# A bidirectional selective scan with a routed FFN gate: the projection kept in float32, one more state scaled on ScalarE, five scan buffers, another prologue

## What is computed

```python
xn = _layernorm(x, axis=-1)

def _selective_scan(x, x_proj_w, dt_proj_w, dt_proj_b, A_log, Dp):
    A = -jnp.exp(A_log)
    dbc = jnp.einsum('bld,nd->bln', x, x_proj_w)
    delta, Bm, Cm = jnp.split(dbc, [DT_RANK, DT_RANK + D_STATE], axis=-1)   # 32, 16, 16
    delta = jax.nn.softplus(jnp.einsum('blr,dr->bld', delta, dt_proj_w) + dt_proj_b)
    deltaA = jnp.exp(delta[..., None] * A)
    BX = delta[..., None] * Bm[:, :, None, :] * x[..., None]
    ...   # h[t] = deltaA[t] * h[t-1] + BX[t] along the tokens
    y = jnp.einsum('blds,bls->bld', hs, Cm)
    return y + Dp * x

s = scan_forward(xn) + scan_backward(xn)
# the FFN, with the expert sel of the row (8 experts, 256 -> 512 -> 256):
h = gelu(einsum('bsh,bhf->bsf', xn, W1[sel]) + b1[sel])
out = (einsum('bsf,bfh->bsh', h, W2[sel]) + b2[sel]) @ Wo + bo
x = x + s * silu(xn + 0.3 * out)
```

## Time and profile before

| | |
|---|---|
| median of 3 runs | 3154.97 us (3154.29 to 3155.58) |
| the profiled execution's own time | 3155.45 us |
| its span | 3153.7 us |
| VectorE busy | 3030.7 us (96%) |
| GpSimd busy | 3013.3 us (96%) |
| ScalarE busy | 2942.1 us (93%) |
| TensorE busy (matmul / weight load) | 2540.5 (81%) / 2013.5 us (64%) |
| mean granted TensorE clock | 0.943 |

### The profile page before, as it was taken

The page is one execution under the profiler, slowest core; times in us unless marked ns, Lnnn a source line. Parts: engine busy times, 40 slices in busy tenths (PEclk is TensorE's granted clock), DMA queues, the critical chain, the costliest instruction groups (busy, mean ns, idle before and its releaser), DMA issues. The chain is left out here.

```text
span 3153.7 us, 49209 instructions
## 1 busy us (share of the span) xinstructions
PE 2540.5 (81%) x15990; PEld 2013.5 (64%) x15990; DVE 3030.7 (96%) x1995; ACT 2942.1 (93%) x5242; POOL 3013.3 (96%) x1486
## 2 busy tenths in 40 slices
PE   7788778888788788788888788887888887887886
PEld 5666666666666666666666666666666665666665
DVE  2899999999999999999999999999999999999998
ACT  4899999999999999999999999999999999999995
POOL 2799999999999999999999999999999999999997
PEclk9999999999999999999999999999999999999998
DMA  5543344443344443444443444443444433444331
GB/s 158 151 123 124 104 130 140 132 126 120 110 129 139 131 118 119 122 131 138 125 122 111 126 139 135 124 121 109 128 142 131 120 121 117 129 139 130 109 121 54
DMA packets 273364, 394.17 MB, mean 125 GB/s; under 512 B 45003, under 2 KB 119508, under 8 KB 273108
## 3 DMA queue, kind: packets, MB, share of 16 engines
q1 hardware_dynamic: 273108, 391.03, 41.4%
HBM read 348.98 MB, written 25.18 MB: 119 GB/s over the span
## 5 line engine op out<-in xcount | busy, mean ns | idle before, releaser
L480 POOL TENSOR_TENSOR bx<-dx,b_sb 128x1024 f32<-128x1024 f32 x576 | 1362.4, 2386 | 22.0 <-DVE hs L861 21.8
L861 DVE TENSOR_TENSOR_SCAN hs<-decay,bx 128x1024 f32<-128x1024 f32 x576 | 1311.7, 2282 | 29.1 <-POOL hc L468 20.8
L468 POOL TENSOR_TENSOR hc<-hs,c_sb 128x1024 f32<-128x1024 f32 x480 | 1133.2, 2371 | 13.5 <-DVE hs L861 12.9
L1093 PE MATMUL y<-ident,hc 128*128 128x128 f32 x8192 | 1112.3, 285 | 36.9 <-DVE hc L840 36.9
L1093 PEld LDWEIGHTS y<-ident,hc 128*128 128x128 f32 x8192 | 977.2, 146 | 151.8 <-DVE hc L840 107.3
L861 DVE TENSOR_TENSOR_SCAN hs<-decay_sb,decay 128x1024 f32<-128x1024 f32 x448 | 1007.3, 2273 | 18.3 <-issue 13.8
L736 ACT ACTIVATE decay<-delta,rate 128x512 f32<-128x512 f32 x1152 | 748.1, 687 | 71.7 <-DVE hs L861 71.3
L594 ACT ACTIVATE dxb<-dxT,btok 128x256 f32<-128x256 f32 x1792 | 763.5, 508 | 0.1
L1068 PE MATMUL decay<-ident,dxb 128*128 128x128 f32 x3584 | 476.5, 276 | 238.3 <-DVE hs L861 219.1
L840 DVE TENSOR_TENSOR hc<-hs,c 128x1024 f32<-128x1024 f32 x544 | 652.0, 1199 | 0.6 <-issue 0.6
L1068 PEld LDWEIGHTS decay<-ident,dxb 128*128 128x128 f32 x3584 | 396.0, 141 | 395.3 <-issue 252.2
(11 more groups left out here) (125 smaller groups left out, 2066.0 us busy)
## 6 DMA issues: line engine op xcount, KB each, us to landing
b_sb<-b_scratch SPq DMA_DIRECT2D x576, 256.0 KB, 3.3
c_sb<-b_scratch SPq DMA_DIRECT2D x480, 256.0 KB, 3.6
xin<-in_L_attn_x_dram SPq DMA_DIRECT2D x32, 512.0 KB, 6.2
w_sb<-in_L_ffn_W_dram SPq DMA_DIRECT2D x32, 512.0 KB, 3.4
w2o_sb<-w2o_scratch SPq DMA_DIRECT2D x32, 512.0 KB
xres<-in_L_attn_x_dram SPq DMA_DIRECT2D x32, 512.0 KB, 5.4
out_dram<-og SPq DMA_DIRECT2D x32, 512.0 KB, 4.3
dbc<-high SPq DMA_DIRECT2D x64, 128.0 KB, 2.3
```

The lines of the kernel that those rows point to most:

```text
L468: nc.gpsimd.tensor_tensor(hc[:, s % RING, :, :], hs[:, s % HSLOTS, :, :], c_sb[:, i % CRING, :].unsqueeze(1).broadcast_to([P, DT, T]), ALU ...
L480: nc.gpsimd.tensor_tensor(bx[:, i % RING, :, :], dx[:, g, :, :], b_sb[:, i % BRING, :].unsqueeze(1).broadcast_to([P, DT, T]), ALU.mult).th ...
L861: V.tensor_tensor_scan(hs[:, s % HSLOTS, :, :].rearrange("p k t -> p (k t)")[:, u], factor.rearrange("p k t -> p (k t)")[:, u], data.rearr ...
L1093: ins = M(yps[:, c, k * P:(k + 1) * P], hc[:, s % RING, k, c * P:(c + 1) * P], ident[:, :], start=False, stop=(s == ADDED[-1]), is_transpo ...
```

## The change

- `high`, `low`, `dbc` and the selector are gone, with the activation, the VectorE subtraction and the four DMAs per row that made them. `projected` gets two buffers, by the row's parity. ScalarE's one copy waits that the stores and the C broadcasts of two rows before are done with it. Expands are one float32 matmul each and the C broadcasts take a column of the identity; both read `projected`.
- State 12 joins `TURNED`, with its scaling at step 8 by the new `SCALED_AT` entries (7 for state 12 and 8 for 13); GpSimd does 17 states of bx in place of 18. dxb has four slots in place of three. The decay of state 8 is made at step 5. The scaling of state 15 moves from step 10 to 11. GpSimd's first log1p of the next row moves from step 25 to 26.
- hs has five slots in place of four, taken in turn across rows.
- In the prologue W2^T has two buffers in hc; the last tokens' load has a semaphore of its own, and ScalarE's work on the row and its first transposed copy stand before that on the last tokens. SyncE reads the router's index after the store of expert 2, not of expert 3. On TensorE the four expands come before expert 4, the bias too, and the hidden parts lie among experts 6 and 7, where they stood before expert 5. Gelu stands before the copies of expert 7 and the second decay, and the dx turns and their copies come behind.

```diff
-    HSLOTS = 4
+    HSLOTS = 5
-    TSLOTS, XSLOTS = 3, 3
+    TSLOTS, XSLOTS = 3, 4
-    LOG1P, STEPSIZE, DX, CUT = (25, 36), (27, 39), (28, 43), (29, 44)
+    LOG1P, STEPSIZE, DX, CUT = (26, 36), (27, 39), (28, 43), (29, 44)
-    TURNED, SCALED_AT, TURN_LEAD = (5, 6, 8, 9, 11, 13, 14, 15, 22, 24, 26, 28, 29, 30), (1, 2, 3, 4, 5, 7, 9, 10, 17, 19, 21, 23, 24, 25), 3
+    TURNED, SCALED_AT, TURN_LEAD = (5, 6, 8, 9, 11, 12, 13, 14, 15, 22, 24, 26, 28, 29, 30), (1, 2, 3, 4, 5, 7, 8, 9, 11, 17, 19, 21, 23, 24, 25), 3
-    AHEAD, AHEAD_NEXT = {14: 22, 15: 24, 16: 26, 23: 28, 26: 29, 27: 30}, {29: 5}
+    AHEAD, AHEAD_NEXT = {5: 8, 14: 22, 15: 24, 16: 26, 23: 28, 26: 29, 27: 30}, {29: 5}
...
-            def high_part(row):
+            def copy_projected(row, par):
                 act.wait_ge(s_pf, row * UNITS + 3)
 
-                wait(act, s_dbc, row * 64)
-                A(high[:, :], fps[:, :], ACT.Copy).then_inc(s_hi, 1)
-
-                wait(act, s_bstored, row * 32)
-                A(projected[:, :], fps[:, :], ACT.Copy).then_inc(s_proj, 1)
+                wait(act, s_bstored, (row - 1) * 32)
+                wait(act, s_cps, (row - 1) * ND)
+                A(projected[:, par, :], fps[:, :], ACT.Copy).then_inc(s_proj, 1)
...
-            def turn_b(row):
-
-                pe.wait_ge(s_lo, row + 1)
+            def turn_b(row, par):
+
                 pe.wait_ge(s_proj, row + 1)
...
-                if q == 0:
-                    pe.wait_ge(s_dbc, row * 64 + 64)
-                M(fps[:, :], dtw_high[:, g, k, :], dbc[:, par, g, :], start=True, stop=False)
-                M(fps[:, :], dtw_low[:, g, k, :], dbc[:, par, g, :], start=False, stop=True).then_inc(s_pf, 1)
+                M(fps[:, :], dtw[:, g, k, :], projected[:, par, :], start=True, stop=True).then_inc(s_pf, 1)
...
-                g, n = s // N, s % N
-                M(cps[:, :], selector[:, N + n:N + n + 1].broadcast_to([P, P]), dbc[:, par, g, :], start=True, stop=True).then_inc(s_cps, 1)
+                at = s // N * 64 + R + N + s % N
+                M(cps[:, :], ident[:, at:at + 1].broadcast_to([P, P]), projected[:, par, :], start=True, stop=True).then_inc(s_cps, 1)
...
             def turn_w2(e):
 
                 pe.wait_ge(s_w2[e % 2], e // 2 * 16 + 16)
+                wait(pe, s_w2Tc, 2 * e)
```

More of the change, by code:

```diff
@@ L167, in mamba_moe_block @@
         w2_in = (w2o_sb, xres)
-        w2T_sb = hc[:, 0, :, :]
-        w2T = w2T_sb.rearrange("p a (j k f) -> p (a j) k f", k=DT, f=P)
+        w2T_sb = [hc[:, a, :, :] for a in range(2)]
+        w2T = [w2T_sb[a].rearrange("p a (j k f) -> p (a j) k f", k=DT, f=P) for a in range(2)]
         w2o_st = (og, zz)
@@ L332, in load_residual, with store_bc @@
                 sp.dma_start(xres[:, :, :], one(x_rows, row)).then_inc(s_xr, 16)
[L334 to L341, removed]
+            def store_bc(row, par):
                 wait_alone(sp, s_proj, row + 1)
                 for g in range(2):
-                    sp.dma_start(b_dram[par, g], projected[64 * g + R:64 * g + 64, :]).then_inc(s_bstored, 16)
+                    sp.dma_start(b_dram[par, g], projected[64 * g + R:64 * g + 64, par, :]).then_inc(s_bstored, 16)
             def load_b(row, par, j):
@@ L418, in body @@
                             load_x(row + 2)
-                        move_bc(row + 1, 1 - par)
+                        store_bc(row + 1, 1 - par)
             rows(body)(sp)
@@ L754, in _ @@
             make_decay(0, 0, 0)
-            for h in range(2):
-                copy_w2o(NE - 1, h)
+            hidden(0, 3)
+            gelu(0)
+            act.preload_act_table_set(exp_ln)
+            copy_w2o(7, 0)
+            copy_w2o(7, 1)
             act.wait_ge(s_w2oc, 2 * NE)
             make_decay(0, 0, 1)
-            gelu(0)
-            act.preload_act_table_set(exp_ln)
+            copy_dxT(0, 0)
+            copy_dxT(0, 1)
             def body(row, par, last):
@@ L804, in mean_variance @@
                     V.bn_aggr(mv[:, c, :], stats[:, c, :]).then_inc(s_mv, 1)
-            def low_part(row):
-                dve.wait_ge(s_proj, row + 1)
-                V.tensor_tensor(low[:, :], fps[:, :], high[:, :], ALU.subtract).then_inc(s_lo, 1)
             def gate_input(row, v):
@@ L930, in _ @@
             V.tensor_copy(bias_part[:, 2, :], bias_rest2[:, :]).then_inc(s_biasc, 1)
-            for e in range(5, NE):
+            for e in range(4, NE):
                 copy_w2T(e)
@@ L1048, in front @@
                 if s == B_TURN:
-                    turn_b(row)
+                    turn_b(row, par)
                 if s in DX_TURN:
@@ L1174, in _ @@
             M(bias_ps[0:NE, 0:D], ones_row[:, 0:NE], bo_row[:, :], start=False, stop=True).then_inc(s_bias, 1)
[L1175 to L1183 removed]
+            turn_w2(4)
+            times_wo(4, 0)
+            times_wo(4, 1)
+            turn_w2(5)
+            times_wo(5, 0)
+            times_wo(5, 1)
+            turn_w2(6)
+            for k in range(DT):
+                ffn_in(0, 0, 0, k)
             times_wo(6, 0)
[L1185 removed]
+            for k in range(DT):
+                ffn_in(0, 0, 1, k)
             times_wo(6, 1)
[L1187 removed]
+            for k in range(DT):
+                ffn_in(0, 0, 2, k)
             turn_w2(7)
+            for k in range(DT):
+                ffn_in(0, 0, 3, k)
             times_wo(7, 0)
             times_wo(7, 1)
+            turn_dx(0, 0, False)
+            turn_dx(0, 1, False)
             pe.wait_ge(s_biasc, 2)
```

212 lines of the change are left out of this document (89 added, 123 removed).

## The result

The changed kernel takes 3162.59 us (median of 9 runs, 3161.47 to 3165.0) where the kernel before took 3154.29 beside it (9 runs, 3152.14 to 3155.58): a ratio of 1.0027 with a 95% interval of 1.0017 to 1.0038. It is slower by 8.3 us. The forecast was 3130 with a range of 3104 to 3158, so it had the wrong sign, and the range did not hold the time.

A forecast was written before the change was run, and what follows sets the result against it. VectorE and GpSimd were taken as full, ScalarE nearly, only TensorE with room. From 3155.45 us, 16 for the prologue and 9 for 31 rows (95.2 us each) came off, giving 3130, range 3104 to 3158.

The forecast's parts named there:

- the hs slot's wait: Steady row: five slots take away VectorE's 0.67 us wait per row for GpSimd to release a slot.
- the prologue: Before the first scans: three waits go, scan of state 2 at 74 to 77 us, 16 us off, bounds 5 and 19.
- state 12, the decay of state 8 ahead: Steady row on ScalarE: VectorE's 0.52 us wait at state 13 goes, a 0.7 us wait at state 14 appears.
- float32 in place of the parts: Steady row: VectorE loses the low part, 0.68 us; longer broadcast and expand make it wait 0.7 us at state 18.
- small waits: Steady row: two small VectorE waits of together 0.2 us go, some 0.4 us appear behind states 14 and 18.
- 1.7 us earlier: Steady row: ScalarE reaches state 13's decay 1.7 us earlier, one decay pair (1.23) and the high copy (0.48) less.
- The half us that was to go: Steady row: VectorE's 0.52 us wait ahead of the scan of state 13, for ScalarE's decay, would be gone.
- the low part's whole 0.68 us: Steady row: VectorE loses the low part between two scans, taken as 0.68 us off its floor.
- C: Row's start: TensorE binds, waits of 2.5 to 3 us before state 6's scan; row 96.5, 3170 us, slower; 13%.
- B: Row's start: longer broadcasts keep TensorE's clock at 2.4 GHz, the wait at state 14 goes; row 94.5, 3108 us; 20%.
- D: Prologue: W2 traffic, the port or the half clock hold it, gaining only 6 us; row 95.4, 3146 us; 17%.
- A: The forecast itself: row 95.2 us, 16 us off the prologue, time 3130 us; 45%.

The follow-up runs named there:

- e5: Kernel before with one constant changed, GpSimd's log1p of the next row at step 26 instead of 25: 3131.15 us, ratio 0.9928.
- e1: Kernel before with the new prologue and the log1p at step 26; parts, fourteen turned states and four hs slots kept: 3120.64 us, ratio 0.9889.
- e2: e1 plus state 12 scaled on ScalarE, with the decay of state 8 made ahead: 3144.72 us, ratio 0.9963.
- e6: Changed kernel with four hs slots in place of five: 3162.27 us, ratio 1.0027.
- e9: e7 with the log1p back at step 25, five hs slots kept: 3106.96 us, ratio 0.9849.
- e10: e9 with four hs slots, so log1p step and slots both as in the kernel before: 3122.98 us, ratio 0.9899.
- e8: e1 with state 13's four scalings made twice on ScalarE, and e2's steps and decay of state 8: 3143.43 us, ratio 0.9963.
- e11: e7 with state 12 scaled on ScalarE again: 3114.87 us, ratio 0.9874.
- e4: Changed kernel with projection and an identity in float32r, so C's broadcast is one instruction; expands stay float32: 3139.31 us, ratio 0.9947.
- e7: Changed kernel with projection and expand weights in float32r, one pass each, no parts, and without state 12 on ScalarE: 3106.21 us, ratio 0.9845.

## Why the prediction was wrong

The runs can be laid in a line from the kernel before to the changed one, each step one part; beside it what the prediction's sum had for that part over 31 rows.

| part | runs | measured | predicted |
|---|---|---|---|
| the hs slot's wait | before to e5 | -22.6 us | -21 (0.67 x 31) |
| the prologue | e5 to e1 | -10.5 | -16 |
| state 12, the decay of state 8 ahead | e1 to e2 | +24.1 | +6 (0.7 - 0.52 at states 14 and 13) |
| float32 in place of the parts | e2 to after | +17.9 | +1 (0.7 at state 18 - 0.68) |
| small waits | | | +6 (0.4 - 0.2) |
| sum | | +8.9 | -24 (-25 as it was rounded there) |

Each ratio is known to about 0.15%, which is 5 us, so the parts are good to a few us each. The step from e2 to the changed kernel also has the fifth hs slot, which e6 found to be worth nothing, and a fourth dxb slot, which no run tried by itself.

**The hs slot: right in size**, and the five slots do take the wait away (e9, e10). What the prediction didn't say is that GpSimd, for which that scan waits, itself waits 1.0 us per row for ScalarE at the log1p, and that the log1p's new step takes both waits away as well.

**State 12: the step that failed is "1.7 us earlier".** ScalarE's own load was right to 0.1 us (92.59). The prediction took the decay of state 8 ahead to fill the wait of 1.29 us, and drew from that and the two activations less a ScalarE that reaches state 13's decay 1.7 us earlier, so that the 0.52 us of VectorE's wait there would go. The wait was filled (0.12 us are left). But two of ScalarE's next instructions read what TensorE makes, and TensorE was not earlier. Order of time in the changed kernel:

```profile
1157.73 2.08 ACT L543 ACTIVATE xn<-xin,shift,rs 128x256 f32<-128x256 f32 x4
...
1160.88 1.91 PE L1059 MATMUL y<-ident,hc 128*128 128x128 f32 x16
...
1162.62 0.60 PE L931 MATMUL front<-ident,xn 128*128 128x128 f32 x4
...
1163.26 0.60 ACT L551 ACTIVATE xnT<-front 128x512 f32<-128x512 f32 x1 [0.62 <-PE front L931]
...
1170.55 1.02 PE L937 MATMUL front<-xnT,wx 128*128 128x512 f32 x2
...
1171.61 0.60 ACT L558 ACTIVATE projected<-front 128x512 f32<-128x512 f32 x1 [0.40 <-PE front L937]
```

The transposes of xn stand on TensorE behind two states' additions to y, whose first operand comes from VectorE. ScalarE had xn ready at 1159.8 and waits 0.62 us for its own work to come back, and 0.40 more for the projection; 0.11 stands ahead of xn itself. So 1.13 of the 1.29 us return as waits, nearly all for TensorE. The added scalings don't shrink, so they come on top. That is the path of e8 too, where ScalarE alone got more. The prediction also counted the scalings up to state 13's decay and not to state 12's: between state 7's decay and that one there now stand four sets and not three, 1.6 us more, less 1.23 for the decay of state 8, and 0.73 us of the waits. In the kernel before it was ready only 0.54 us ahead of its scan. So VectorE waits 0.5 us at state 12 as it did at state 13 in the earlier trace rows, and at state 14 besides:

```profile
1169.88 1.33 ACT L666 ACTIVATE decay_sb<-delta,rate 128x512 f32<-128x512 f32 x2
...
1171.29 4.50 DVE L836 TENSOR_TENSOR_SCAN hs<-decay_sb,decay 128x1024 f32<-128x1024 f32 x2 [0.49 <-issue]
...
1174.92 1.32 ACT L666 ACTIVATE decay_sb<-delta,rate 128x512 f32<-128x512 f32 x2
...
1176.33 2.29 DVE L836 TENSOR_TENSOR_SCAN hs<-decay_sb,decay 128x1024 f32<-128x1024 f32 x1 [0.54 <-ACT decay_sb L666]
```

State 14's 0.54 was forecast, as 0.7, with the right engine named. The half us that was to go, and stayed, is 15 us of the error (0.5 x 30).

**Float32: the place was right, the size too small.** At state 18, to be laid beside the earlier trace rows:

```profile
1183.10 1.12 PE L1042 MATMUL c<-projected,ident 128*128 128x512 f32 x2
...
1184.06 1.91 PE L1059 MATMUL y<-ident,hc 128*128 128x128 f32 x16
...
1185.81 1.02 PE L978 MATMUL front<-projected,dtw 128*128 128x512 f32 x2
...
1186.87 0.69 ACT L586 ACTIVATE ex<-front,dtb 128x512 f32<-128x512 f32 x1 [0.69 <-PE front L978]
...
1188.02 1.30 ACT L666 ACTIVATE decay<-delta,rate 128x512 f32<-128x512 f32 x2
...
1189.41 2.29 DVE L836 TENSOR_TENSOR_SCAN hs<-decay,bx 128x1024 f32<-128x1024 f32 x1 [0.86 <-issue]
```

From the broadcast's start to the additions it is 0.96 us (0.34 before, 0.86 said), from the expand's start to ScalarE 1.06 (0.74 before, 1.05 said), and VectorE waits 0.86 (0.7 said). The same place in e11, in one pass:

```profile
1071.13 0.48 PE L983 MATMUL front<-projected,dtw 128*128 128x512 f32 x1
...
1071.65 0.69 ACT L589 ACTIVATE ex<-front,dtb 128x512 f32<-128x512 f32 x1
...
1072.31 4.46 DVE L841 TENSOR_TENSOR_SCAN hs<-decay,bx 128x1024 f32<-128x1024 f32 x2
```

The expand's result is there 0.52 us after its start, ScalarE doesn't wait, VectorE neither, and the wait behind at state 20 (0.28 us per row in the changed kernel and 0.27 in e4) is gone too. What the prediction missed is twofold. It credited the low part's whole 0.68 us, while VectorE's busy time fell by 0.4 (94.05 to 93.64): instructions that follow each other overlap by 0.1 us in the records (4.8 us per row before, 4.3 now), and an instruction that goes or a wait that appears takes such an overlap with it, so a floor made by subtracting durations was 0.3 us too low. And it treated ScalarE as outside this chain: its wait for the expand went from 0.29 to 0.69 us per row, on an engine that by then had no time to give.

So the row came out at 96.2 in place of 95.2: 0.5 from the wait that didn't go, 0.3 from the lost overlap, and 0.2 from small waits and from rows taken as 95.5 that are 95.56 on average. States 14 and 18 together came out as forecast (0.53 and 0.86 for 0.7 and 0.7).

**The prologue: right in direction, 5 us short.** The chain of the first scans (the prediction said 31 for the first expand, 64 for the end of the products, 74 to 77 for the scan of state 2):

```profile
30.91 0.69 ACT L586 ACTIVATE ex<-front,dtb 128x512 f32<-128x512 f32 x1 [0.26 <-PE front L978]
...
43.39 5.26 PE L1080 MATMUL decay<-decay_sb,hc 128*128 128x256 f32 x16 [1.60 <-DVE hc L845]
...
65.66 3.62 PE L1080 MATMUL decay<-decay_sb,hc 128*128 128x256 f32 x16
...
66.57 1.28 ACT L618 ACT_TABLE_LOAD   x1
...
69.79 1.28 ACT L738 ACT_TABLE_LOAD   x1
...
73.61 2.29 DVE L836 TENSOR_TENSOR_SCAN hs<-decay,bx 128x1024 f32<-128x1024 f32 x1 [4.10 <-ACT decay L666]
...
78.14 2.28 DVE L836 TENSOR_TENSOR_SCAN hs<-decay,bx 128x1024 f32<-128x1024 f32 x1
```

The first expand came a little early, the wait for W1 is gone, and gelu with its tables takes the 4.5 us. The products end at 69.3 and not at 64. One of them, in a stretch with a mean clock of 0.86, took 5.26 us where its neighbours take 3.6 to 3.7, after 1.60 us of waiting for VectorE's copy, and from there to the last TensorE has hardly a gap. That is 3.2 of the 5.3 us; the rest wasn't traced. The two stretches:

```profile
43.00:55.00 12.00, 11.27 (x50) 9.31 (x51) 3.16 (x6) 5.15 (x7) 11.73 (x6) 0.86 0.70 220
55.00:65.00 10.00, 10.00 (x38) 6.37 (x37) 1.64 (x3) 5.74 (x9) 4.72 (x3) 1.00 0.31 107
```

Then the first row gave 5.1 us back. VectorE waits there for 4.1 us for decay 1, which now stands behind gelu and its tables, 1.6 for broadcasts of C, 2.5 at states 11, 12, 18 and 20, and 5.5 for the FFN's output; the kernel before waited for 3.0 at its first decays, 1.0 at states 13 and 31, and 4.2 for the FFN. That is 13.7 against 8.2 us. Not all of it is the prologue's: in e1's profile, with the same prologue, row 0 takes 101.8 us and no product waits for a broadcast, against 100.2 in e5's. How much is, stays open, since e1's profiled execution was 5 us shorter than its median.

**The rivals.** *C* gave 3170, near the time, but by another way: states 5 and 6 don't wait, and no product waits for c in a steady row. *B's* condition came true, its result not. TensorE is granted 1.00 in the rows, and the eight passes at the row's start take 1.89 us as they would by B, not 3.71 as in the earlier trace rows:

```profile
1154.80 1.89 PE L1003 MATMUL front<-w2o_sb,hT 128*128 128x256 f32 x8
```

The row is longer all the same. e7 has the shortest row of all at a mean clock of 0.94. The half clock had cost little where it stood, since no scan of the kernel before waited there. *D*: the prologue's -10.5 lies between A's -16 and D's -6, as the scan of state 2, at 78.1, lies between 77 and 82. Half of D came true, and it explains 5 of the 33 us.

**What stays open.** That the xn transposes' place in TensorE's order is what state 12 pays for was read from the trace, not tried: no run moved them. Why its price is 24, 18 and 9 us in three surroundings wasn't separated either (GpSimd, which state 12 relieves, is busy for over 99% of the rows in e1 and e7 alike); in e11 it still has both waits, 0.50 and 0.53, in each row. And of the prologue's parts none was run alone.

## What to carry to other kernels

When work is moved onto an engine because a wait there seems to have room, follow that engine's next instructions to their producers. If they read what a third engine makes, and that one is no earlier, the gap comes back one or two instructions later and the added work is paid in full or by half. A part that saves time on the engine that looks full (a low part here) can lose it on the loop of two engines that look free, if it makes one step of that loop longer: 1.02 in place of 0.50 us per broadcast and expand cost 48 us in 3160, though TensorE had a tenth of its time left. And when a change has two cures for one wait, count it once, and try each alone: one constant, the step of the log1p, gave 22.6 us by itself.

## What the runs showed of the hardware

- A float32 matmul of 512 columns is busy for 1.02 us against 0.50 for float32r. On TensorE's path it weighs more: from its start to that of the instruction behind it, 0.96 against 0.34 us at state 18, and 0.86 against 0.32 in the median of the steady rows' broadcasts with no gap behind them. By the Trainium skill (FP8 and Floating Point Precision, TensorE Precision Notes) true FP32 takes four passes. Against float32r the busy times give a factor of 2.0 and the distances one of 2.7 to 2.8, and TensorE was busy for 86.0 us a row, not for over 104. The prediction's product of four and 0.505 us counted a float32r matmul as one pass. How many it is no run here shows, so the four passes are neither borne out nor refuted; only the product is.
- TensorE's granted clock was 1.00 through all rows with the float32 broadcasts in (86.0 us busy of 96.2), and 0.93 to 0.96 in every kernel whose broadcasts take one instruction. It bought nothing here: the kernel with the highest clock is the slowest.
- In the new prologue the bias subtractions ran while GpSimd stood idle and took 0.41 us each; in the earlier trace rows one took 2.59 beside a busy GpSimd. Not each is slow there: the one of 51.84, which reads the bank c, took 0.41 beside GpSimd too. GpSimd's first instruction after 33.75 us of waiting stands right behind them.

```profile
41.24 0.41 DVE L894 TENSOR_TENSOR dxb<-c,bias_part 8x256 f32<-8x256 f32 x1
...
42.01 0.41 DVE L898 TENSOR_TENSOR dxb<-dxb,bias_part 8x256 f32<-8x256 f32 x1
...
43.05 2.34 POOL L441 TENSOR_TENSOR lg<-lg,ex 128x1024 f32<-128x1024 f32 x1 [33.75 <-ACT lg L608]
```
